# A 128 KB copy moved from the tail to the head of the sync engine's step, in a pipelined attention stage with routing

## The reference

```python
x = _layernorm(x + _L0_attn_ref(x, ...), axis=-1)
x = _layernorm(x + _L0_ffn_ref(x, ...), axis=-1)

# _L0_ffn_ref
logits = jnp.einsum('bsd,de->bse', x, router_w)
top_logits, indices = jax.lax.top_k(logits, K)          # K = 2 of E = 8
weights = jax.nn.softmax(top_logits, axis=-1)
```

## Time and profile before

| what | value |
|---|---|
| time, median of 3 runs | 1658.11 us (1652.84 to 1662.07) |
| time of the profiled execution | 1666.16 us, its span 1664.4 us |
| PE busy | 1182.4 us, 71% of the span |
| DVE busy | 957.6 us, 58% |
| ACT busy | 616.2 us, 37% |
| POOL busy | 448.7 us, 27% |
| mean granted TensorE clock | 0.813 of full speed |
| PE's steps 5 to 18 of layer 0's pipeline | about 112 to 404 us of the span |

### The profile page before, as it was taken

One profiled execution on the slowest core, in us unless ns is written; L12 is line 12 of the kernel. 1 busy time (PEld: TensorE's weight loads), 2 busy tenths in 40 slices (PEclk: granted clock), 3 DMA queues, 4 the chain that ended last, 5 costly groups with the idle time before them and its releaser, 6 DMA issues.

```text
span 1664.4 us, 31729 instructions
## 1 busy us (share of the span) xinstructions
PE 1182.4 (71%) x9203; PEld 850.3 (51%) x9203; DVE 957.6 (58%) x3461; ACT 616.2 (37%) x1352; POOL 448.7 (27%) x614
## 2 busy tenths in 40 slices
PE   1488998889288884567644788889886799438920
PEld 1255554555177773455533566767654566325710
DVE  4477877777422222587753465666647678762245
ACT  1055555556033331223521454555555223113400
POOL 5111333333400002783351011111103211340046
PEclk9788878879599998688765899899998589558965
DMA  4222333220356654211002222222101000115512
GB/s 119 73 66 62 81 78 78 75 63 25 128 152 171 170 159 146 63 55 42 32 10 75 70 64 68 65 67 66 38 22 35 22 20 19 34 55 153 160 51 66
DMA packets 90533, 124.79 MB, mean 75 GB/s; under 512 B 13361, under 2 KB 73522, under 8 KB 87218
## 3 DMA queue, kind: packets, MB, share of 16 engines
q1 hardware_dynamic: 84274, 110.74, 23.3%
q0 software_dynamic: 6144, 12.60, 2.6%
HBM read 72.18 MB, written 33.55 MB: 64 GB/s over the span
## 4 chain that ended last, share of the span: by engine, by line
PE 37%; DMA 20%; DVE 15%; issue 13%; POOL 9%; SPq 3%; ACT 2%; DVEq 0%; POOLq 0%; ACTq 0%
DMA we<-in_pack 6%; PE po L437 5%; DMA xr<-xg 4%; PE po L1495 4%; POOL yr L1567 3%; DMA scr<-parts 2%; PE pt L400 2%; PE pt L1489 2%; PE pt L397 2%; DVE xg L335 2%; POOL rstd L328 2%; PE pm L1489 2%; DMA xs<-xg 2%; DMA yr<-result,at_row 2%; PE pm L418 2%
## 5 line engine op out<-in xcount | busy, mean ns | idle before, releaser
L606 DVE TENSOR_REDUCE mx<-pm 128x2 f32<-128x512 f32 (+1 forms) x512 | 308.2, 620 | 249.1 <-PE pm L424 140.0
L559 ACT ACTIVATE ex<-pt 128x512 f32<-128x512 f32 (+1 forms) x512 | 271.5, 544 | 261.2 <-PE pt L397 131.2
L1567 POOL DMA_INDIRECT yr<-result,at_row x96 | 95.3, 993 | 330.1 <-issue 328.3
L325 POOL TENSOR_SCALAR ve<-mv 128x2 f32<-128x2 f32 x96 | 25.2, 262 | 584.3 <-DVE mv L319 584.1
L437 PE MATMUL po<-ex,va 128*32 128x256 f32 (+1 forms) x2048 | 165.0, 397 | 3.6 <-ACT ob L568 3.6
L400 PE MATMUL pt<-hide_k,ident 128*128 128x128 bf16 x512 | 98.6, 230 | 38.0 <-issue 29.0
L397 PE MATMUL pt<-qs,ks 99*128 99x256 bf16 x512 | 112.7, 309 | 16.2 <-DMA qs<-mt 11.6
L418 PE MATMUL pm<-ks,qs 96*128 96x256 bf16 x512 | 116.9, 316 | 6.0 <-DVE mx L606 5.3
L304 PE MATMUL p<-ident,xs 128*128 128x128 f32 x112 | 40.8, 364 | 103.8 <-DMA xs<-xg 100.5
L309 ACT COPY xt<-p 128x256 f32<-128x256 f32 x112 | 41.8, 373 | 196.2 <-PE p L305 196.1
L1495 PE MATMUL po<-he,we 128*128 128x256 f32 (+1 forms) x448 | 112.9, 395 | 0.5 <-DVE yt L1531 0.4
(11 more groups left out here) (283 smaller groups left out, 2890.4 us busy)
## 6 DMA issues: line engine op xcount, KB each, us to landing
we<-in_pack SPq DMA_DIRECT2D x40, 514.5 KB, 4.1
xs<-xg SPq DMA_DIRECT2D x112, 128.0 KB, 2.0
scr<-parts SPq DMA_DIRECT2D x32, 384.0 KB
we<-in_pack SPq DMA_DIRECT2D x16, 512.0 KB, 4.2
qs<-scr SPq DMA_DIRECT2D x32, 192.0 KB
ks<-scr SPq DMA_DIRECT2D x32, 192.0 KB
xe<-sorted SPq DMA_DIRECT2D x40, 128.0 KB, 2.0
result<-ye SPq DMA_DIRECT2D x40, 128.0 KB, 3.7
```

The source lines that it names most:

```text
L559: nc.scalar.activation(ex[j % 2][:, 2 * u:2 * u + 2, lo:S], pt[:, u, :].rearrange("p (b k) -> p b k", k=S)[:, :, lo:S], ACT.Exp).then_inc( ...
L606: nc.vector.tensor_reduce(mx[q.slot % 2][:, qt, 4 * b + 2 * u:4 * b + 2 * u + 2], pm[:, u, :].rearrange("p (b k) -> p b k", k=S)[:, :, 0:h ...
L1567: pool.indirect_dma_start(out=yr[q.slot][:, t, i, :], out_offset=None, in_=rows, in_offset=bass.IndirectOffsetOnAxis(ap=at_row[q.slot][:, ...
```

## The change

The three statements that copy `xr` move from the end of SP's step to its beginning. Nothing else changes, and no other engine's list of instructions differs.

```diff
         def heads_sync(sp, a, g, n, routed):
             def step(at):
+                if routed and (q := at(6)):
+                    wait_apart(sp, ln_x, 2 * (n + q.n + 1), passed)
+                    wait_apart(sp, scattered[q.slot], 64 * q.turn, passed)
+                    sp.dma_start(xr[q.slot][:, :, :], xg[:, bass.ds(2 * q.n, 2), :]).then_inc(xr_loaded[q.slot], 16)
                 if (q := at(0)):
                     load_x(sp, q, g, n)
                 if (q := at(4)):
...
                                      ).then_inc(stacked[q.slot], 16)
-                if routed and (q := at(6)):
-                    wait_apart(sp, ln_x, 2 * (n + q.n + 1), passed)
-                    wait_apart(sp, scattered[q.slot], 64 * q.turn, passed)
-                    sp.dma_start(xr[q.slot][:, :, :], xg[:, bass.ds(2 * q.n, 2), :]).then_inc(xr_loaded[q.slot], 16)
             sweep(sp, 7, step, lead=SLOTS if routed else 0)
```

## The result

The changed kernel takes 1700.22 us (median of 4 runs, 1698.95 to 1704.39), the kernel before 1658.61 (4 runs, 1652.84 to 1662.07). The ratio is 1.0239 (95% interval 1.0206 to 1.0272): slower by 2.4%. The profiled execution took 1704.39 us.

The account below looks back on a forecast made before the run. It took the bound to be PE's wait for the xr copy, queued behind the stacks' 16.8 us, at 22.4 us a step. Terms of +3.3, +27.1 and +8.9 summed to +39.3 on the median 1658, giving 1697 us, range 1668 to 1710.

Parts of the forecast that it names:

- What is removed: PE's waits for the xr copy, given as 37.1 us in 16, vanish; the copy lands in about 2 us.
- L335's end to (4, 0), 4.77: From the normed sequence complete to PE's restart at part (4, 0), behind two copies and the maxima rows: 4.77 us.
- (4, 0) to L304, 11.72: From PE's part (4, 0) to the next L304, with the clock lowered after a stall: 11.72 us, between 8.83 and 12.54.
- rival A: The stall moves to part (4, 0) but the clock mostly recovers; 1664 to 1682 us; chance 15 in 100.
- L304 to L335's end, 8.66: Last stretch of a step, from L304 to the normed sequence complete, taken from the trace: 8.66 us.
- Step 5, +3.3: PE reaches part (4, 0) of step 5 at 124.85 in place of 121.58, 3.3 us later.
- Ten steps, +27.1: From part (4, 0) of step 5 to that of step 15: 251.5 us in place of 224.4.
- Steps 16 to 18, +8.9: These steps have no xs copy, so 4.01 us in place of 4.77; they lose 2.0, 4.0 and 2.9 us.
- The rest, 0: Later steps have no maxima rows; layers 1 to 3, the experts and layer 2's attention are untouched, so nothing is added.
- B: The removed wait is replaced by nothing, a step falls to some 20 us; faster, 1634 us; chance 6 in 100.
- C: Gain and new wait cancel, no difference; needs a step of 22.4 us or less; chance 5 in 100.
- D: Above the upper bound: late xs copy or parts, and stacks colliding with the next step's maxima rows; chance 6 in 100.

Follow-up runs that it names:

- e1: Kernel before with only the wait for the normed sequence added at the head of SP's step, the xr copy left at the tail; 1693.42 us, ratio 1.0119.
- e3: The change with the xs copy and the maxima rows issued ahead of the wait and the xr copy; 1653.79 us, ratio 0.9885.
- f2: The kernel before run again with a profile of its own, nothing changed; 1655.98 us, ratio 0.9991.
- f1: The change run again, nothing else changed; 1701.67 us, ratio 1.0256 to the kernel before.
- g1: The change with layer 0's six stack DMAs replaced by twelve of 8 rows each, the same bytes; 1688.28 us, ratio 1.0172 to the kernel before.
- f4: Kernel before with the xr copy moved between the write of the parts to scr and SP's wait for that write, ahead of the stack DMAs; 1642.33 us, ratio 0.9905.
- g2: Kernel before with layer 0's six stack DMAs replaced by twelve of 8 rows each; 1631.35 us, ratio 0.9839.
- g4: Kernel before with the xr copy between the parts' write and the stack DMAs, and twelve stack DMAs in layer 0; 1617.99 us, ratio 0.9764.
- e4: The change with the maxima rows issued by ACT right behind its copy to mt, not by SP; 1658.68 us, ratio 0.9906 to the kernel before.
- f3: Kernel before with the xr copy issued by ACT on its own queue at the start of its step; 1645.30 us, ratio 0.9922.

## Why the prediction was right

The forecast was 1697 us (1668 to 1710), measured 1700.22. Step by step:

- **What is removed.** As said: next to no idle time for `xr`, landing in 2.1 us. The 37.1 us that the prediction gives for PE were misread, PE's own waits are 25.0; no term of the sum was made from them.
- **L335's end to (4, 0), 4.77.** Measured in steps 6 to 14: 4.71 to 5.22, mean 4.87. In step 12 the four pieces are 0.15, 0.81, 0.92 and 3.34, against 0.16, 0.76, 0.76 and 3.09. The 0.5 us for the queue in the upper bound came from no row; the distance exceeded 4.77 by 0.1 in the mean and by 0.45 at most. PE's waits that follow from it are 2.8 to 5.1 us in the 14 steps, where 3 to 4.6 were named. The fixed cost of about 2.0 us, which the Trainium skill gives (DMA: Bandwidth & Descriptors, Anatomy of one DMA) for a DMA that GpSimd issues, would have made the total some 4 us lower. These DMAs are issued by SP, and from the first of the two to PE's start it is 3.19 to 3.38 in these steps, so the row of the trace gave the better term.
- **That this distance is a wait.** e1, without the moved copy, keeps most of it (4.00 in the step shown), and e3, with the rows ahead of the wait, loses it. So it is the wait at the head, shown from both sides.
- **(4, 0) to L304, 11.72.** This was the uncertain term, chosen by the row with the nearest stall. Measured 10.90 to 12.47, mean 11.59. The granted clock was 0.63 to 0.72 there in each step, which rival A denied. **L304 to L335's end, 8.66**: 8.65 in most of them. The step came to 25.00 against 25.15.
- **Step 5, +3.3.** Measured −0.2 (121.40 against 121.58). The distance is there, 121.40 − (115.33 + 1.37) = 4.70 in that execution, but L335 ended at 116.70 where the earlier trace rows have 120.08. The sum took the early steps of one execution as given; they came 3.4 us earlier in the next. In the other profiles with six stack DMAs in layer 0, this L335 ends between 116.5 and 118.6, so the execution before was the late one. With f2 and f1 the same term is 120.12 to 122.27, +2.2.

The timeline of the kernel after at step 5, from which these numbers are:

```profile
115.33 1.37 DVE L335 TENSOR_SCALAR xg<-res,mv,rstd 128x128 f32<-128x128 f32 x2
...
116.85 0.57 SPq L356 DMA_DIRECT2D xr<-xg  x1
```

- **Ten steps, +27.1.** Measured 248.2 − 224.4 = +23.8. The first of them took 23.2, and the last is shorter by a detail: the `xs` copy is missing already ahead of (4, 0) of step 15 (3.85 after L335), one step earlier than the sum had it.
- **Steps 16 to 18, +8.9.** Measured 67.2 − 56.8 = +10.4, with 3.82 to 4.05 for the 4.01.
- **The rest, 0.** Measured 1265.8 − 1261.6 = +4.2, and +7.5 for f1 against f2. "Later steps have no maxima rows" is right, but the last stall still costs clock behind itself, which the sum left out. From (4, 0) of step 18 to the end of the next L335 the change takes 14.10 us and the kernel before 11.69 (14.11 and 11.68 in f1 and f2), for the same 111 products of PE at a granted clock of 0.76 instead of 1.00. That is +2.4 in both pairs. What is left, +1.8 and +5.1, was not traced to a cause, and may be what executions differ by.
- **The sum, +39.3.** Measured −0.2 + 23.8 + 10.4 + 4.2 = +38.2 in span. Four terms missed: step 5 by −3.5 and the ten steps by −3.3, steps 16 to 18 by +1.5 and the rest by +4.2. They nearly cancel. So the mechanism and the size of a step were right, and that the sum came within 1.1 us is in part luck.
- **The rivals.** A fell by the clock. B named its condition, the normed sequence complete no later than `mt`; it came 4.6 us later (290.12 against 285.51), the same distance as before, and B's mechanism with the condition met by order is e3, whose step of 21.43 is 1.2 below the kernel before, half of the 2.4 that B promised, because the maxima rows then meet the stacks' tail. C needed a step of 22.4 and got 25.0. D fell by g1.

## What to carry to other kernels

On an engine that issues in order, a moved DMA takes its wait along, and everything behind it then waits for the newest data: before moving it ahead, set the time at which its data is complete against the time at which each item queued behind it is ready. Move such a copy to a place where its wait is already satisfied, best into a wait that the queue has anyway (f4), rather than to the place where it is first possible. And when a small transfer is late behind large ones, look at the large ones too: splitting them by rows shortened the tail for everything behind them (g2, g4: 14.7 us, not 16.8). And a PE wait of a few microseconds costs its length plus the clock after it: the same stretch from (4, 0) to L304 took 8.83 us at a granted clock of 1.00 and 10.9 to 12.5 at 0.63 to 0.72.

## What the runs showed that was not expected

- ACT's queue is no way past SP's load. Two 12 KB DMAs on it came 17.0 us after the first stack DMA (e4), where 16.8 to 16.9 are needed on SP's queue itself; a 128 KB copy on it came after 13.4 (f3). Why the one got past a part of the load and the other not is open.
- While 768 KB loaded in six DMAs of 24, 16 and 8 rows, some 5 of 16 DMA engines were busy, and 2 to 3 in the two windows shown; with twelve DMAs of 8 rows some 9, at a rate that was little higher (88 GB/s, not 76; the tail 14.7 us, not 16.8). More engines did not bring time in proportion.
- With SP's wait gone the pipeline alternates between steps of about 18.5 and 24.5 us from L304 to L304 (e3, f4): the stacks' tail hits the maxima rows in every other step. A mean step hides this.
